# A decoder block's attention stage: the layer norms' shifts on GpSimd behind the third features, another order of VectorE's work, and X added by an identity product that ScalarE copies back

## The reference

```python
x = x + attn(layernorm(x))            # causal linear attention, 16 heads of 8
x = x + xattn(layernorm(x), ctx)      # autocorrelation attention, top 5 lags
x = x + ffn(layernorm(x))             # 8 experts, 2 per row

def attn(x):
    q, k = feature_map(x @ wq + bq), feature_map(x @ wk + bk)   # x + 1 where x > 0, else exp(x)
    v = x @ wv + bv
    # for every head: S and z are running sums over the rows of the sequence
    S = cumsum(k outer v); z = cumsum(k)
    return ((q @ S) / (q . z + 1e-6)) @ wo + bo
```

## Time and profile before

| | us |
|---|---|
| median of 3 runs | 626.69 (625.57 to 626.80) |
| profiled execution | 626.32 |
| its span, first to last instruction | 624.1 |
| TensorE busy in the span | 556.2 |
| VectorE busy | 504.1 |
| ScalarE busy | 417.6 |
| GpSimd busy | 407.6 |
| attention stage, about | 0 to 270 |

### The profile page before, as it was taken

One profiled execution on the slowest core, in us unless ns is written; L12 is line 12 of the kernel. 1 busy time (PEld: TensorE's weight loads), 2 busy tenths in 40 slices (PEclk: granted clock), 3 DMA queues, 4 the chain that ended last, 5 costly groups with the idle time before them and its releaser, 6 DMA issues.

```text
span 624.1 us, 16569 instructions
## 1 busy us (share of the span) xinstructions
PE 556.2 (89%) x4286; PEld 407.8 (65%) x4287; DVE 504.1 (81%) x1506; ACT 417.6 (67%) x1188; POOL 407.6 (65%) x459
## 2 busy tenths in 40 slices
PE   4888999999999998878899786899999999999993
PEld 1333444444444444445888544799999999999993
DVE  4489999999999999874578988466887878877883
ACT  3556878888888775532888502445887888878882
POOL 2778888888888888112877501764566766757762
PEclk9979999999999999899999969999999999999998
DMA  5510111111161112362568480221111111111110
GB/s 153 187 50 2 35 35 36 35 34 34 34 101 34 34 37 65 67 137 57 159 196 206 78 137 5 59 51 38 35 50 51 47 44 47 52 40 51 52 45 22
DMA packets 49973, 40.99 MB, mean 66 GB/s; under 512 B 21971, under 2 KB 40278, under 8 KB 49926
## 3 DMA queue, kind: packets, MB, share of 16 engines
q1 hardware_dynamic: 44150, 29.68, 19.5%
q0 software_dynamic: 4960, 10.49, 6.4%
q10 hardware_dynamic: 816, 0.26, 0.2%
HBM read 27.54 MB, written 12.88 MB: 65 GB/s over the span
## 4 chain that ended last, share of the span: by engine, by line
PE 55%; ACT 16%; DVE 10%; issue 10%; POOL 4%; DMA 3%; ACTq 0%; SPq 0%; DVEq 0%; POOLq 0%
PE bank L1349 30%; PE run L1349 19%; ACT xh L678 4%; PE bank L1353 4%; ACT xs L780 2%; ACT ex L656 2%; DMA shared<-xs_d,row_u 2%; ACT nb_a L675 2%; PE run L1616 1%; ACT ex L661 1%; DVE mean_early L1057 1%; ACT xT L649 1%; PE run L1540 1%; DMA ct<-in_ctx_r 1%; ACT rl L657 1%
## 5 line engine op out<-in xcount | busy, mean ns | idle before, releaser
L616 POOL DMA_INDIRECT shared<-xs_d,row_u x91 | 87.8, 965 | 62.6 <-DVE row_u L1247 31.6
L549 POOL TENSOR_TENSOR shared<-v,qk 128x1024 f32<-128x1024 f32 x64 | 125.0, 1953 | 2.8
L623 POOL DMA_INDIRECT out_x<-shared x64 | 63.5, 992 | 48.2 <-DVE shared L1319 22.1
L899 DVE TENSOR_TENSOR R<-run,qk 128x1024 f32<-128x1024 f32 x64 | 77.5, 1210 | 12.5 <-PE run L1349 11.0
L1349 PE MATMUL bank<-wqkv,xT 128*64 128x128 f32 (+1 forms) x384 | 70.5, 353 | 15.5 <-ACT v L659 10.8
L1349 PEld LDWEIGHTS bank<-wqkv,xT 128*64 128x64 f32 (+1 forms) x384 | 33.4, 159 | 72.1 <-issue 37.4
L909 DVE TENSOR_REDUCE num<-R 128x128 f32<-128x1024 f32 x64 | 77.2, 1206 | 1.1
L1349 PE MATMUL run<-shared,tris_s 64*64 64x512 f32 x512 | 73.3, 644 | 0.0
L809 ACT ACTIVATE shared<-run,scale_s 128x128 f32<-128x128 f32 (+1 forms) x78 | 30.0, 385 | 41.5 <-PE run L1616 41.5
L540 POOL TENSOR_TENSOR qk<-ex,rl 128x256 f32<-128x256 f32 x64 | 46.5, 727 | 11.0 <-DVE mv_a L884 7.5
L656 ACT ACTIVATE ex<-bank 128x256 f32<-128x256 f32 x64 | 24.1, 376 | 28.9 <-PE bank L1349 28.9
(11 more groups left out here) (277 smaller groups left out, 1425.1 us busy)
## 6 DMA issues: line engine op xcount, KB each, us to landing
xs_d<-xs SPq DMA_DIRECT2D x16, 270.0 KB, 5.2
X<-in_x SPq DMA_DIRECT2D x16, 256.0 KB, 2.7
ct<-in_ctx_t SPq DMA_DIRECT2D x16, 256.0 KB, 3.0
ct<-in_ctx_r SPq DMA_DIRECT2D x16, 256.0 KB, 3.7
gram_d<-gd SPq DMA_DIRECT2D x14, 256.0 KB, 2.4
w_s<-in_w_experts SPq DMA_DIRECT2D x8, 384.0 KB, 3.9
circ<-prob_d SPq DMA_DIRECT2D x30, 64.0 KB, 2.8
shared<-xs_d,row_u POOLq DMA_INDIRECT x91, 2.6
```

What stands on the lines that cost most here:

```text
L549: nc.gpsimd.tensor_tensor(outer[k].rearrange("p (h e d) -> p h e d", h=H, e=D), vv.unsqueeze(3).broadcast_to([P, H, D, D]), kk.unsqueeze(2 ...
L616: nc.gpsimd.indirect_dma_start(xg[q], None, xs_d[:, :], bass.IndirectOffsetOnAxis(ap=rows, axis=0)).then_inc(xg_in[q], 16)
L623: nc.gpsimd.indirect_dma_start(out[:, :], bass.IndirectOffsetOnAxis(ap=xg[(NXI + j) % NX][:, DEST:DEST + 1].bitcast(U32), axis=0), yg[q], ...
L899: nc.vector.tensor_tensor(R[:, 0:D * E].rearrange("p (h e d) -> p h e d", h=H, e=D), run[k % 2][:].rearrange("p (h e d) -> p h e d", h=H, ...
```

## The change

GpSimd computes mean times root and then 1 minus it for each of the two norms, in one instruction each for the whole group, and ScalarE's instructions for mr and nb are gone. On GpSimd variance, root, product and shift of group a0 stand in one piece behind the third features, and those of the c group at the end of the slot, with their product and shift in the next slot. X is added to the attention's result inside bank 6, by a matmul of the identity with the group's 512 columns of X, and ScalarE copies the bank into X; VectorE's addition is gone. VectorE takes statistics and moments of a0 around the key dots and those of c at the end of the slot. The two small instructions by which VectorE made nb for the last half group are replaced by a wait for GpSimd's.

```diff
 # GpSimd
+            def mean_times_root(g, p, mv, rs, rs_sem, mr, mr_sem, nb_sem):
+
+                pool.wait_ge(rs_sem, g + 1)
+                need(pool, nb_sem, g)
+                nc.gpsimd.tensor_tensor(mr[:], mv[p][:, :, 0], rs[p][:], ALU.mult).then_inc(mr_sem, 1)
+
+            def shift(g, p, mr, mr_sem, nb, nb_sem, normed):
+
+                pool.wait_ge(mr_sem, g + 1)
+                need(pool, normed, GT * (g - 1))
+                settle(pool)
+                nc.gpsimd.tensor_scalar(nb[p][:], mr[:], -1.0, 1.0, ALU.mult, ALU.add).then_inc(nb_sem, 1)
...
                 if a1:
                     features(*a1, 0)
+                if d:
+                    mean_times_root(d[0], d[1], mv_c, rs_c, c_rs, mr_c, c_mr, c_nb)
+                if a1:
+                    outer_product(*a1, 0)
+                if d:
+                    shift(d[0], d[1], mr_c, c_mr, nb_c, c_nb, d_xh)
+                if a1:
+                    features(*a1, 1)
+                    outer_product(*a1, 1)
+                    features(*a1, 2)
                 if a0:
                     variance(*of_a)
-                if a1:
-                    outer_product(*a1, 0)
-                    features(*a1, 1)
                 if a0:
                     root(*of_a)
-                if a1:
-                    outer_product(*a1, 1)
-                    features(*a1, 2)
-                if c:
-                    variance(*of_c)
+                    mean_times_root(a0[0], a0[1], mv_a, rs_a, a_rs, mr_a, a_mr, a_nb)
+                    shift(a0[0], a0[1], mr_a, a_mr, nb_a, a_nb, a_xh)
                 if a1:
                     outer_product(*a1, 2)
                     features(*a1, 3)
                 if c:
-                    root(*of_c)
+                    variance(*of_c)
                 if a1:
                     outer_product(*a1, 3)
+                if c:
+                    root(*of_c)
...
 # ScalarE
+            def add_attention(g, p, r):
+                act.wait_ge(c_y, g + 1)
+                settle(act)
+                nc.scalar.activation(X[:, bass.ds(GT * g, GT), :].rearrange("p t e -> p (t e)"), bank[6][:], ACT.Copy
+                                     ).then_inc(c_x1, 1)
+
+            def norm(g, p, rs, nb, nb_sem, dst, dst_sem, own=GT):
+                act.wait_ge(nb_sem, g + 1)
+                settle(act)
                 for k in range(own):
-                    nc.scalar.activation(nb[p][:, k:k + 1], mr[:, k:k + 1], ACT.Copy, bias=1.0, scale=rs[p][:, k:k + 1]).then_inc(nb_sem, 1)
-                for k in range(own):
-                    act.wait_ge(nb_sem, GT * g + k + 1)
                     nc.scalar.activation(dst[:, k, :], X[:, bass.ds(GT * g + k, 1), :].rearrange("p a b -> p (a b)"),
                                          ACT.Identity, bias=nb[p][:, k:k + 1], scale=rs[p][:, k:k + 1]).then_inc(dst_sem, 1)
...
-                if d:
-                    negative_mean(d[0], d[1], mv_c, c_mv, mr_c, c_mr)
...
                     nc.scalar.activation(k2T[:], bank[4][:], ACT.Identity, bias=wkk[:, E:E + 1]).then_inc(d_kT, 1)
+                if c:
+                    add_attention(*c)
+                if d:
                     act.wait_ge(d_tr, d[0] + 1)
                     nc.scalar.activation(x2T[:], bank[5][:], ACT.Copy).then_inc(d_xT, 1)
...
-                    negative_mean(g, p, mv_a, a_mv, mr_a, a_mr)
-                    norm(g, p, rs_a, a_rs, mr_a, a_mr, nb_a, a_nb, xh, a_xh)
+                    norm(g, p, rs_a, nb_a, a_nb, xh, a_xh)
...
 # VectorE
                 if c:
                     quotients(*c)
+                if a0:
+                    g, p, r = a0
+                    dve.wait_ge(x_in[p], 16 * r + 16)
+                    stats(g, p, st_a, a_st, mv_a, a_mv, a_mr, 1)
                 if b:
                     key_dots(*b)
                 if a0:
-                    g, p, r = a0
-                    dve.wait_ge(x_in[p], 16 * r + 16)
-                    stats(g, p, st_a, a_st, mv_a, a_mv, a_nb, GT)
+                    moments(a0[0], a0[1], st_a, a_st, mv_a, a_mv, a_mr, 1)
                 if b:
                     sum_heads(*b, 1)
                     sum_dots(*b)
-                if a0:
-                    moments(a0[0], a0[1], st_a, a_st, mv_a, a_mv, a_nb, GT)
...
                 if b:
                     times_q(*b, 2)
-                if c:
-                    add_attention(*c)
-                if b:
                     sum_heads(*b, 2)
-                if c:
-                    dve.wait_ge(c_x1, c[0] + 1)
-                    stats(c[0], c[1], st_c, c_st, mv_c, c_mv, c_nb, GT)
                 if b:
                     times_q(*b, 3)
                 if c:
-                    moments(c[0], c[1], st_c, c_st, mv_c, c_mv, c_nb, GT)
+                    dve.wait_ge(c_x1, c[0] + 1)
+                    stats(c[0], c[1], st_c, c_st, mv_c, c_mv, c_mr, 1)
                 if b:
                     sum_heads(*b, 3)
+                if c:
+                    moments(c[0], c[1], st_c, c_st, mv_c, c_mv, c_mr, 1)
...
 # TensorE
                     mm(bank[6][:], ones3[:], b_o, True, False)
+                    mm(bank[6][:], id_s[:], X[:, bass.ds(GT * g, GT), :], False, False)
                     for k in range(GT):
                         last = mm(bank[6][:, k * P:(k + 1) * P], oT[:, k * P:(k + 1) * P], wo_s[:], False, k == GT - 1)
```

More of the change, by code:

```diff
@@ L146, in build @@
         xh2 = sb("xh2", [P, GT, E])
-        last_mr = sb("last_mr", [P, GT // 2])
         x2T, k2T = sb("x2T", [P, GW]), sb("k2T", [P, GW])
@@ L271, in build @@
         gram_out = sems("gram_out", 2)
-        last_nb = sem("last_nb")
         diag_in, mean_ch, mean_mm, prob_e = sem("diag_in"), sem("mean_ch"), sem("mean_mm"), sem("prob_e")
@@ L553, in slot @@
             def slot(n, i):
-                a0, a1, c = stage(n, i, 2), stage(n, i, 1), stage(n, i, -1)
+                a0, a1, c, d = (stage(n, i, k) for k in (2, 1, -1, -2))
                 of_a = a0 and (a0[0], a0[1], mv_a, a_mv, ve_a, a_ve, rs_a, a_rs, a_xh)
@@ L703, in slot @@
                     need(act, d_tr, g)
-                    norm(g, p, rs_c, c_rs, mr_c, c_mr, nb_c, c_nb, xh2, d_xh, GT // 2 if i is None and g == NG - 1 else GT)
+                    norm(g, p, rs_c, nb_c, c_nb, xh2, d_xh, GT // 2 if i is None and g == NG - 1 else GT)
                 if d:
@@ L956, in quotients @@
                     rden.unsqueeze(2).broadcast_to([P, GT * H, D]), ALU.mult).then_inc(c_on, 1)
[L958 to L963, removed]
             def slot(n, i):
-                a0, a1, b, c = (stage(n, i, s) for s in (2, 1, 0, -1))
+                a0, b, c = (stage(n, i, k) for k in (2, 0, -1))
                 if b:
@@ L1031, in last_rows @@
             def last_rows(g, p):
[L1032 to L1038, removed]
+                dve.wait_ge(c_nb, g + 1)
                 dve.wait_ge(d_tr, g)
```

## The result

The changed kernel takes **688.9 us** (median of 4 runs, 680.5 to 696.4) against 626.1 of the kernel before, 1.100 by these medians. The ratio 1.092, with a 95% interval of 1.083 to 1.102, comes from the two faster runs alone, 680.5 and 686.3, since the other two, the profiled one among them, lie over 1.5% above the fastest. The forecast was 662 with 654 to 678 about it, and even the fastest run lies above that. The direction came, and so did the wait that was named; the size did not. The runs differ by 16 us among themselves. Two executions of this kernel have a trace: the one of 691.5 us has nine slots lengthened by a fall of the clock, one of 680.6 us (experiment 12) has five, so most of the spread is put down to their number.

A forecast was written before the change was run, and what follows sets the result against it. A per-slot ring of TensorE and ScalarE work (14.88 us) bounds the kernel; late shift 1.75 plus product 0.96 over twelve slots give +32.5, filling +1, draining +2: 626.3 + 35.5 = 662 us, range 654 to 678.

The forecast's parts named there:

- the wait that was named: ScalarE idle before xh, released by GpSimd's nb_a behind the third features: about 2.7 us per slot.
- The sum: Whole kernel: +32.5 us in twelve full slots, +1 filling, +2 draining, in all +35.5 us, giving 662.
- The ring: One attention slot: TensorE and ScalarE work closes into a chain of waits that sets the pace, 14.88 us.
- four links: First to third projection 6.74 us; on to x2T 1.71; x2T to xh 2.71; xh to next first projection 3.72.
- The late shift: GpSimd's shift behind the third features: ScalarE's x2T to xh becomes 4.46 us instead of 2.71, +1.75 per slot.
- product to shift: GpSimd, mean times root to 1 minus it, within the coming group's chain before xh: 0.29 us.
- The product: TensorE's f32 identity matmul with X, between first and third projection: +0.96 us per slot.
- nb_c done: GpSimd's c-group shift in the next slot ends about 3.4 us after the first Exp, before xh2 needs it: costs nothing.
- Filling and draining: Three slots before the full ones +1 us (bounds 0 to 8), three after them +2 (bounds 0 to 5).
- rival A: TensorE's idle before xh halves its clock in three to five slots, 3.4 us or less each: 670 to 678; chance 0.24.
- B: TensorE's work sets the pace, the shift coming in time: -0.1 us per slot, 625, no change; chance 0.05.
- C: VectorE sets the pace and loses 0.92 us per slot with its add and wait: 614 to 618; chance 0.05.

The follow-up runs named there:

- experiment 12: The changed kernel again, unaltered: 686.3 us (680.6 to 692.9), 1.100 of the kernel before.
- experiment 3: The changed kernel with eight bf16 matmuls put ahead of TensorE's wait for xh in slots that have all stages: 666.9 us.
- experiment 2: The changed kernel with the coming group's variance, root, product and shift behind GpSimd's second features instead of the third: 631.9 us.
- experiment 1: The kernel before with only the identity matmul, ScalarE's copy of X, and one wait for all four nb ahead of xh: 639.4 us.
- experiments 4 and 10: Changed kernel without identity matmul and ScalarE's copy, VectorE's addition back: 669.1 us; the same with eight matmuls ahead of TensorE's wait for xh: 662.8 us.
- experiment 9: The kernel before with only the coming group's product and shift on GpSimd, with variance and root behind the second features: 616.9 us.

## Why the prediction was right in its mechanism and wrong in its size

**The sum.** It gave +35.5 us. With the clock held the change costs 40.5, and as it stands 62.8. The difference of 22 is the fall of the clock, which the sum put at nothing; the other 5 are handoffs and the ends of the stage.

**The ring: right.** The four links sum to the measured pace before (14.88) and after, once the clock is held (17.82, experiment 3). The wait has the releaser named, the place named, and about the length named (3.11 us; forecast 2.7). Moving the chain by one place takes 57 us away again (experiment 2).

**The late shift: right, a little small.** Forecast +1.75 us with bounds 1.7 to 2.0, measured 4.87 - 2.71 = 2.16, outside the bounds. The terms that were too small are the handoff of 0.07 us, taken from the earlier trace rows, a slot that is written out, and product to shift, taken from the earlier trace rows. Inside the loop the features start 0.24 us after the Exp ends, and shift's end to xh is 0.22; in the written-out slots these are 0.07 and 0.12. Product to shift is 0.42 instead of 0.29 in both kinds of slot. These are an Exp and its features in a written-out slot of the changed kernel, 69.06 to 69.13, 0.07 us (ScalarE, then GpSimd):

```profile
68.62 0.44 ACT L678 ACTIVATE ex<-ex 128x256 f32<-128x256 f32 x1
```

```profile
69.13 0.73 POOL L551 TENSOR_TENSOR qk<-ex,rl 128x256 f32<-128x256 f32 x1 [1.74 <-ACT ex L678]
```

**The product: right in place and size.** Forecast 0.96 from ct with wkk, measured 0.86. The Trainium skill (FP8 and Floating Point Precision, TensorE Precision Notes) names four passes, an estimated 0.85 us for 512 columns at 2.4 GHz, and the trace agrees with that. On its own it is all on the ring (experiment 1). Beside the late shift it costs only 0.4, because a second ring through nb_c stands close behind (experiments 4 and 10). I had put that one at nothing: the prediction has nb_c done while ScalarE is still in the second evacuation, but ScalarE waits 0.93 us for it there (experiment 3). This hardly changes the forecast of the whole, but it does the split: the late shift alone is worth 2.6 us a slot (17.46 against 14.84), and the parts do not add.

**Filling and draining: small by 3 us.** Experiment 3 against the kernel before: the twelve full slots +34.8 (forecast 32.5), the three ahead of them +2.2 (forecast 1), from the last xT to the reduction after the stage +3.7 over before (forecast 2), all from the two profiles. Together with a start 1.4 us later that is 42.1 in the profiles and 40.5 in the medians, where 35.5 was forecast: 667 instead of 662, within the range.

**The clock: the step that failed.** Of the 63 us, 22 are falls of the granted clock: 688.9 with them, 666.9 with the wait filled (16 by the mean of its two shortest runs). The forecast's sum had no term for it. It stood as rival A, at 0.24, and priced at 670 to 678. Two things in it were wrong. I weighed a piece of 2.0 us against one seen fall after 2.30, and held it for too short; the piece became 2.50, since the late shift was undersized. And I let it happen in three to five slots. It happened in nine in one execution (2.6 us for each, 20.46 - 17.82) and in five in the other, three of these by 1.0 to 1.2 us only. The price of one fall, 3.4 us or somewhat less, was too high if anything: the one looked at lasts 6.7 us, and its slot is 2.6 longer. The high end of the range was cut by the small number of slots I gave it, not by a row. A fixed wait in a loop comes again in every slot; the honest bound was all twelve at 2.6 or more, some 31 us, and a high end of 693.

**The other rivals.** B and C, no change or faster, needed the shift ahead of ScalarE's den. The trace shows it behind: ScalarE waits 3.11 us for nb_a. C's view of VectorE as the next bound does hold once the ring is cut: experiment 9 runs at VectorE's pace. The Trainium skill (Perfetto Trace Analysis, Identifying the Most-Contended Engine) would have it first; here relieving VectorE gave nothing while the ring was longer than its work (experiment 1).

## What to carry to other kernels

When several engines are busy 80 to 96% each, lay their queues of one period side by side and close the ring: if its links sum to the period, an edit can be priced by whether it lies on a link, as long as no second ring is close behind. Moving small work from the engine on the ring to one with time to spare is only a gain if what stands ahead of it in that engine's queue is done before the ring needs the result: behind the second features it was, behind the third it was not. Move just the part that is on the ring. And if a change makes TensorE wait as long in every period as a trace shows before a fall of its clock (here 2.3 us), price a fall for every period, or fill the wait.

## What had not been expected

- The granted clock fell from 1.00 to 0.50 after 2.3 to 2.6 us of idle TensorE in a period of 17.4 to 20.5, in some slots and not in others with the same wait. In the profiled execution a wait of 2.82 us, ahead of the loop, had no fall behind it. With 1.75 us of idle few falls were left, with 0.7 none. What decides between two equal slots was not settled.
- Eight useless matmuls in each full slot made the changed kernel 22 us faster by the medians.
- The two handoffs of the lengthened link, Exp to features and nb_a to xh, take 0.07 and 0.12 us in every written-out slot and 0.24 and 0.22 in every slot of the loop; nb_c to xh2, elsewhere in the slot, takes 0.11 and 0.20 in turn in the loop of experiment 3. In the loop the counts waited for and the addresses depend on the loop's index; that this is the reason is not shown. Over one handoff it is little, and a ring can have several.
- With both norms' shifts on GpSimd and the coming group's early, the gain is 0.7 to 0.9%; with only the coming group's there it is 1.6%. In the first of these TensorE waits 0.58 us for xh2, which waits for GpSimd's nb_c, and in the second that wait is gone. The two kernels also differ in where the c group's variance and root stand, and the two were not told apart.
